# A two-layer graph network on one core: the setup of constants rewritten, sixteen gathers moved into the node pass, and its output rows written in two halves

## The reference, cut to what matters

```python
def _sage_mean(h, src, dst, W_self, W_neigh, b):
    agg = segment_sum(h[src], dst, 50000)
    mean_neigh = agg / maximum(deg, 1.0)[:, None]
    return h @ W_self + mean_neigh @ W_neigh + b
h  = _sage_mean(relu(_sage_mean(x, ..., W_self0, W_neigh0, b0)), ..., W_self1, W_neigh1, b1)
x1 = _layernorm(x + h)
# attention over the edges with q, k + e, v + e (four heads of 128), + x1 @ Wskip + bskip,
# layer norm with ln_g and ln_b, @ Wlin + blin, elu(lin + x1)
x2 = _layernorm(x1 + elu(lin + x1))
```

## Time and profile before

| what | value |
|---|---|
| median of 3 runs | 1757.79 us (1755.62 to 1760.14) |
| the profiled execution, its own time | 1751.26 us |
| its span | 1749.4 us |
| granted TensorE clock, mean of the span | 0.970 |
| PE busy | 1524.3 us (87%) |
| PEld busy | 1024.5 us (59%) |
| DVE busy | 1327.1 us (76%) |
| ACT busy | 1160.0 us (66%) |
| POOL busy | 1041.2 us (60%) |
| DMA | 206.77 MB, mean 118 GB/s |

### The profile page before, as it was taken

How to read it: one execution, slowest core, us unless ns; L and a number is a source line. 1 busy time by engine, 2 the same in 40 slices (tenths; PEclk the granted TensorE clock), 3 DMA queues, 4 the chain that set the end, 5 groups by cost and what they waited for, 6 DMA issues and landing times. The chain is left out here.

```text
span 1749.4 us, 34139 instructions
## 1 busy us (share of the span) xinstructions
PE 1524.3 (87%) x7745; PEld 1024.5 (59%) x7745; DVE 1327.1 (76%) x6197; ACT 1160.0 (66%) x3125; POOL 1041.2 (60%) x1038
## 2 busy tenths in 40 slices
PE   3599999999999998999688867999999999999872
PEld 2477777777777776777455543555555555455441
DVE  4799999999999996656366653777777777777762
ACT  0499999999999995333255541666666666666662
POOL 4688888868888773664455526455555555555320
PEclk9899999999999999999899988999999999999995
DMA  2356566544444442332388853233222232333210
GB/s 79 109 152 158 153 160 154 151 154 144 149 142 148 139 146 74 85 84 70 116 268 271 273 173 80 78 84 85 83 84 84 84 85 79 82 83 85 59 36 4
DMA packets 178820, 206.77 MB, mean 118 GB/s; under 512 B 36607, under 2 KB 104666, under 8 KB 178703
## 3 DMA queue, kind: packets, MB, share of 16 engines
q1 hardware_dynamic: 151502, 169.25, 31.5%
q0 software_dynamic: 27200, 36.26, 9.0%
HBM read 107.47 MB, written 106.49 MB: 122 GB/s over the span
## 5 line engine op out<-in xcount | busy, mean ns | idle before, releaser
L1307 POOL DMA_INDIRECT big<-x_tab,look x196 | 199.6, 1019 | 97.6 <-issue 56.1
L1324 POOL DMA_INDIRECT out_dram<-big,idx x98 | 99.2, 1013 | 259.1 <-DVE big L1640 126.3
L700 PE MATMUL pb<-MG_s,big 128*128 128x256 f32 x832 | 207.4, 392 | 41.5 <-issue 30.7
L700 PEld LDWEIGHTS pb<-MG_s,big 128*128 128x128 f32 x832 | 149.5, 189 | 143.7 <-issue 95.2
L725 ACT ACTIVATE big<-big 128x128 f32<-128x128 f32 x416 | 170.0, 481 | 0.0
L820 POOL TENSOR_TENSOR big<-big,cl 128x512 f32<-128x512 f32 x104 | 133.3, 1282 | 49.8 <-ACT big L749 40.5
L682 PE MATMUL pb<-C_s,big 128*128 128x128 f32 x832 | 161.6, 276 | 0.0
L683 PE MATMUL pb<-Ws1c_s,big 128*128 128x128 f32 x832 | 161.3, 276 | 0.0
L1057 POOL DMA_INDIRECT big<-h1e_tab,hidx x98 | 97.9, 999 | 103.9 <-PE pb L937 45.0
L334 POOL DMA_INDIRECT a_xs<-in_x_dram,idx x98 | 102.3, 1044 | 86.7 <-issue 47.6
L1408 PEld LDWEIGHTS pb<-Wg_s,big 128*128 128x128 f32 x784 | 95.8, 192 | 98.1 <-ACT big L1480 95.8
(11 more groups left out here) (345 smaller groups left out, 4015.1 us busy)
## 6 DMA issues: line engine op xcount, KB each, us to landing
big<-in_x_dram SPq DMA_DIRECT2D x104, 256.0 KB
x_tab<-big SPq DMA_DIRECT2D x98, 256.0 KB
out_dram<-big SPq DMA_DIRECT2D x98, 256.0 KB
ve_tab<-c_ve SPq DMA_DIRECT2D x98, 256.0 KB
c_ve<-ve_tab SPq DMA_DIRECT2D x98, 256.0 KB
h1e_tab<-a_rows SPq DMA_DIRECT2D x25, 256.0 KB
x_tab<-a_rows SPq DMA_DIRECT2D x25, 256.0 KB
big<-eT_tab SPq DMA_DIRECT2D x98, 64.0 KB
```

Source lines behind the costliest of these rows:

```text
L700: t = pe.matmul(o, b_x1T[:, r * P:(r + 1) * P], MG_s[:], start=True, stop=True)
L1307: g.indirect_dma_start(out=o, out_offset=None, in_=x1_tab, in_offset=bass.IndirectOffsetOnAxis(ap=look[:, a, j:j + 1], axis=0), bounds_che ...
```

## The change

Setup: the index rows go out first on SP's queue, the vectors and the larger weights on ACT's queue, and each group has its own semaphore, so that a consumer waits for its group only. The three 256 KB broadcasts of the biases become three rows of 2 KB, which a matmul with a column of 1/D spreads over the partitions. ACT takes the additions of the bias columns, Wg_s, and the copies of Wskip, Wv, Aqk and Aqe out of PSUM from DVE. The PSUM memset goes to the front, and the 10 us memset of POOL behind the last signal that others wait for. Gathers: none in setup and none ahead of the node pass; one in every sixth turn of it (16 in all). Output rows: rows 0 and 1 stay in place, rows 2 and 3 follow the Relu.

```diff
-            for o, i in ((Ws0_s, Ws0), (Wn0_s, Wn0), (Ws1_s, Ws1), (Wn1_s, Wn1), (Wv_s, Wv), (We_s, We),
-                         (Wskip_s, Wskip)):
-                ld(o[:], i)
...
             sp.wait_ge(s_sg, 1)
...
+            ld = load_on(sp, s_li, "index")
             full = NT - 1
             ld(rows_i[0:full, 0, :], dst[0:full * P].rearrange("(t p) -> t p", p=P))
...
-            for o, v in ((set_t, bskip), (set_u, bv), (set_v, be)):
-                ld(o, v.rearrange("(a n) -> a n", a=1).to_broadcast([P, HC]))
...
+            ld = load_on(sp, s_ld, "later")
+            ld(Ws1_s[:], Ws1)
...
+        LOADS = dict(skip=1, lin=1, index=7, rows=10, later=14)
...
+        def setup_act(act):
+            load_on(act, s_lf, "skip")(Wskip_s[:], Wskip)
+            act.preload_act_table_set(ACT_SET)
+            act.wait_ge(s_sg, 1)
+            ld = load_on(act, s_lv, "rows")
+            for r, v in ((18, bskip), (2, bq), (6, bk), (10, bv), (14, be), (22, ln_g), (26, ln_b)):
+                ld(vrow[r:r + 4, :], v.rearrange("(a n) -> a n", n=P))
...
+            ld = load_on(act, s_ld, "later")
+            for r, v in ((0, bskip), (1, bv), (2, be)):
+                ld(set_t[r:r + 1, :], v.rearrange("(a n) -> a n", a=1))
+            ld(set_q, Wq)
...
+            heads_plus(set_sT, 4, 28)
+            w("q")
+            heads_plus(set_qT, 1, 12)
+            w("k")
+            heads_plus(set_kT, 2, 20)
...
+            p("skip")
+            act.activation(Wskip_s[:], pb[6][:], ACT.Copy).then_inc(s_sa, 1)
...
         def setup_pool(g):
...
-            g.wait_ge(s_sg, 7)
-            g.wait_ge(s_sv, vm["idx0"])
-            for s in range(2):
-                gather_src(g, s)
+            g.memset(big[:, b_ghost:b_small_end], 0.0)
...
         def setup_pe(pe):
...
+            pe.matmul(pb[6][:], C_s[:], Wskip_s[:], start=True, stop=False)
+            pe.matmul(pb[6][:], set_one[0:3, :], set_t[0:3, :], start=False, stop=True).then_inc(s_sp, 1)
...
         def b_act(act):
...
-                    for r in range(R):
-                        t = act.activation(b_o[u % 2][:, r * D:(r + 1) * D], b_w[u % 2][:, r * D:(r + 1) * D],
-                                           ACT.Identity, scale=brs3[:, r:r + 1], bias=b_nm3[:, r:r + 1])
-                    t.then_inc(step("b_o"), 1)
+                    for r in range(R // 2):
+                        rows_out(act, u, r)
...
                     act.activation(b_h1T, PH[:], ACT.Relu, bias=b0x[:, 0:1]).then_inc(step("b_h1"), 1)
+
+                    for r in range(R // 2, R):
+                        t = rows_out(act, u, r)
+                    t.then_inc(step("b_o"), 1)
...
         def b_pool(g):
             credit(g, "b_x1c")
-            for s in range(2, 4):
-                gather_src(g, s)
             g.wait_ge(s_red, 16)
...
                     node_row(it)
+                if it % 6 == 5 and it < 96:
+                    gather_src(g, it // 6 // R, it // 6 % R)
```

More of the change, by code:

```diff
@@ L291, in gnn_kernel, with bcast, load_on, ld @@
         s_look = sem("s_look")
-        LOADS = []
+        counts = {n: [] for n in ("skip", "lin", "index", "rows", "later")}
+        def bcast(v, n):
+            return v.rearrange("(a n) -> a n", a=1).to_broadcast([P, n])
+        def load_on(eng, s, what):
+            def ld(o, i):
+                counts[what].append(1)
+                eng.dma_start(o, i).then_inc(s, 16)
+            return ld
         def setup_sync(sp):
@@ new lines, in setup_pe @@
+            pe.wait_ge(s_sg, 3)
+            pe.wait_ge(s_lv, 16 * LOADS["rows"])
+            pe.transpose(pb[0][:, 0:P], vrow, ident[:]).then_inc(s_sp, 1)
+            w("rep1")
+            pe.transpose(pb[7][:, 0:P], rows_f[:, 0, P - 1:P].to_broadcast([P, P]), ident[:]).then_inc(s_sp, 1)
+            for c in range(3):
+                t = pe.transpose(pb[5][:, c * P:(c + 1) * P], rows_f[:, c, :], ident[:])
+            t.then_inc(s_sp, 1)
+            w("sc")
+            four_heads(4, set_sc)
@@ new lines, in setup_pe @@
+            w("vcol")
+            pe.matmul(pb[6][:, 0:H], ones_t, vcol[:, 18:22]).then_inc(s_sp, 1)
+            pe.wait_ge(s_ld, 16 * LOADS["later"])
+            four_heads(1, set_q)
+            four_heads(2, set_k)
+            four_heads(3, We_s[:])
+            a("s")
+            a("wg")
+            sum_heads(pb[0][:, P:2 * P], lambda h: set_sT[:, h, :], lambda h: Wg_s[:, h, :])
+            sum_heads(pb[0][:, 2 * P:3 * P], lambda h: set_sT[:, h, :], lambda h: set_sT[:, h, :]).then_inc(s_sp, 1)
@@ L590, in setup_dve @@
+            v.tensor_tensor(crow[:], pb[7][:, 2 * P:3 * P], set_b[:, D:2 * D], ALU.add)
             v.tensor_scalar(nb0[:], set_b[:, 0:D], -1.0, None, ALU.mult)
-            d("crow", v.tensor_tensor(crow[:], pb[7][:, P:2 * P], set_b[:, D:2 * D], ALU.add))
+            d("cl", v.tensor_tensor(b0x[:], vcol[:, 0:1], pb[7][:, 3 * P:3 * P + 1], ALU.subtract))
+            w("cl")
+            v.wait_ge(s_sa, am["skip"])
+            for b in pb[6:8]:
+                v.memset(b[:].rearrange("p (a d) -> p a d", a=2)[:, :, 0:D], 0.0)
@@ L706, in gnn_kernel, with rows_out @@
         brs1, brs2, brs3 = (b_rs[:, 4 * k:4 * k + 4] for k in range(3))
+        def rows_out(act, u, r):
+            return act.activation(b_o[u % 2][:, r * D:(r + 1) * D], b_w[u % 2][:, r * D:(r + 1) * D],
+                                  ACT.Identity, scale=brs3[:, r:r + 1], bias=b_nm3[:, r:r + 1])
         def b_act(act):
@@ L943, in a_pool @@
                 after(g, "a_pmT", s - 4)
[L944 removed]
+                for r in range(min(R, NT - R * s)):
+                    gather_src(g, s, r)
         def a_dve(v):
```

277 lines of the change are left out of this document (125 added, 152 removed).

## The result

The changed kernel takes 1738.55 us (median of 4 runs, 1737.43 to 1740.29), the kernel before 1756.84 us (4 runs) beside it: ratio 0.9894, 95% interval 0.9877 to 0.9911. That is 18.3 us faster, inside the range of 1717 to 1743 us, though 7.5 us above the 1731 us forecast. The profiled execution took 1740.29 us, its span is 1738.3 us (before 1751.26 and 1749.4).

A forecast was written before the change was run, and what follows sets the result against it. DVE was taken as the bound after the setup's load wait, a PE and ACT ring as the node pass's. Terms -24.3 - 3 - 11.1 + 12 = -26.4 us gave 1725 us profiled, 1731 us against the median; range 1717 to 1743.

The forecast's parts named there:

- The setup: Stage ahead of the node pass: earlier DVE start and shorter DVE chain, end at 30.5 against 54.84 us, -24.3 us.
- DVE's start: Setup: index rows loaded first let DVE start at 12 us instead of 23.15, bounds 10 and 16.
- the third rival: Setup bound by data: DVE starts at 16 us and waits again for later loads, 1737.5 us in all; chance 8%.
- the one-engine rule: Index loads in the setup: 97 partitions would use one DMA engine, putting DVE's start nearer to 14 than 10 us.
- a DVE wait for ACT: Sign that the forecast is wrong: DVE waiting in the setup for ACT, whose copies should hide behind the degrees.
- The start of the node pass: First three turns: with the setup gathers gone POOL is on time and DVE isn't stalled, -3 us.
- The halves: Output rows in two halves shorten the node pass ring; turns fall from 5.871 to DVE's 5.76 us, -11.1 us.
- second rival: The ring doesn't shorten, turns stay at 5.87 us, stalls are partly recovered, gathers cost 10 us: 1740.5 us; chance 17%.
- The gathers: Sixteen gathers in the node pass make x1c late and stall DVE, twelve by 0.6 and four by 1.2: +12 us.
- The rival in which they are absorbed: POOL's slack or shorter waits in its node pass turn take up the gathers: 1719 us; chance 18%.
- x1c out of step: First half of the node pass: POOL's lag never heals, x1c meets L794 every turn, 1.09 us each: 1774 us; chance 4%.
- Stages a, c and d, "untouched": Stages outside setup and node pass: the forecast expected no change in them.

The follow-up runs named there:

- e8: The changed kernel with each load of 97 index rows split into one of 96 and one of 1: 1741.25 us, ratio 0.9916.
- e7: The changed kernel with PE's small products for the degrees ahead of those for Wskip, Wv, Aqk and Aqe: 1735.99 us, ratio 0.9883.
- e4: The kernel before with nothing but the output rows in halves: 1719.59 us, ratio 0.9951.
- e3: The changed kernel with all four output rows ahead of the x1T copy again, gathers unchanged: 1714.13 us, ratio 0.9915.
- e6: The changed kernel with eight gathers in the setup and eight in turns 49 to 51 and 101 to 103: 1727.18 us, ratio 0.9831.
- e10: The same kernel as e6, run once more on the chip of e9: 1724.3 us, ratio 0.9844.
- e2: The changed kernel with its sixteen gathers in turns 49 to 51 and 101 to 103, where POOL has time: 1704.70 us, ratio 0.9867.
- e9: The changed kernel with the edits of e6, e7, e8, degree-row transposes moved up, and the memset in pieces over DVE, ACT and POOL: 1720.38 us, ratio 0.9828.
- e5: The changed kernel once more, no edit, beside the kernel before: 1741.0 us, ratio 0.9902.
- e1: The kernel before once more, no edit, profiled on another chip: 1729.03 us.

## Why the prediction was right, and where it was off

**The setup, -24.3 said, -16.1 measured.** Right in kind: DVE starts on the index rows while the weights still travel, and its chain is shorter. The term was mis-sized by 8.2 us, and outside its bound of 18 at that. Three parts make it up:
- DVE's start, 12 us said, 15.35 measured. The 12 were 1.5 us until SP starts, 8 for the set and 2 for ACT's loads beside it, rounded up. SP started at 1.41 us and the set took 13.9 us from there, so the term for what runs beside it was short by some 4 us. It is the first half of the third rival (a start at 16 us); its second half, a wait of DVE for later loads, didn't come. The forecast said that by the one-engine rule the start would be nearer to 14 than to 10 us, and took 12. e8 settles that the data are late because of the 97-row form: with 96 rows, and ACT's loads beside them as before, they are there at 6.87 us. No run takes ACT's loads away from the 97-row form, so that they are what stretched the set from 8 to 13.9 us is argued, not shown. The Trainium skill ("DMA: Bandwidth & Descriptors", on why a DMA increments its semaphore by 16) says that the number of DMA engines must divide the number of partitions; the trace and e8 agree.
- The cast stood 1.4 us behind POOL's memset (1.75 less 0.36). The forecast had "half a microsecond for meeting POOL's memset" and PE together. It had applied the exclusion in the node pass, from three rows, and not in the setup, where the diff moves a 10 us memset beside the start of the chain.
- The wait of 3.75 us for PE. The forecast checked ACT's sets against the cover of the degrees, but not how much PE has to do, nor in which order: the small products stand behind skip, v, A and Be, and PE works through these without a gap until 33.79 us, when DVE has been ready since 30.07. It named a DVE wait for ACT as a sign of error; it was a wait for PE's own work. e7 puts the small products first, and the wait at L607 is gone; that DVE then stood as long at L633 is for the most part PE's half clock (3.2 of 3.63 us).

Together 3.35 + 1.4 + 3.75 = 8.5 us; the rest of the chain was 0.3 us shorter than said, which leaves the 8.2. The forecast's own sum has a slip in it: 31.7 - 13.6 + 0.4 is 18.5 us, not 18.0, and 19.0 with the half microsecond. Against that the rest of the chain was 0.8 us shorter, so the slip hid half a microsecond of it.

**The start of the node pass, -3 said, -3.05 measured** in the first three turns, and the first load to the first L831 another 0.9 us shorter. Right, mechanism and size: no row of L815 or L835 is stretched in these turns any more, and the halves can't have done it (22.9 us in e4). One row fits the reading only in part: the L774 of 1.97 us in the earlier trace rows starts at 77.49 us, 0.63 us before the addition that it ends with.

**The halves, -11.1 said.** The common turn is 5.76 us as said, with DVE as its bound. Alone (e4) they give 7.7 us on a chip where the turns of before were 5.85. But as a part of this change they are worth about nothing (e3). The two terms aren't additive: the forecast put the 10 us of stalls on top of the shortened ring, and only its second rival said that a stall is partly recovered in a ring that is longer than DVE's work. It is recovered for the most part, 8.5 of 10.4 us. The node pass's 100 turns gained 1.3 us net, where the forecast's terms give -11.1 + 12 = +0.9. That the sum came out right is luck: its two terms were added as if neither touched the other, and the halves' term, a tenth of a microsecond in every turn, was nearly empty beside the gathers.

**The gathers, +12 said, 10.1 measured.** 12 turns of 0.63 and 4 of 1.23 us, where 0.6 and 1.2 were said: this is the step that came out most exactly. The size was 12 x 0.6 + 4 x 1.2 taken in full; the row of 0.15 that each replaces was not taken off, which is the difference (16 x 0.15 = 2.4, less 0.03 us in each of the sixteen). The rival in which they are absorbed fell for this kernel, though with whole rows it nearly holds (1.9 us net in e3), and that of x1c out of step fell too: each stall gave POOL its lag back.

**Stages a, c and d, "untouched".** Not so. The gap behind the pass grew by 5.1 us, which no rival had; 3.76 of them are POOL's longer drain, and e6 and e10 take those away by moving eight gathers out. Stage c's 4.5 us arise around two pauses of PE, whose cause is open, below. All told the traces give -11.1 us and the medians -18.3, against -26.4 said. The 7.2 us between trace and median are the distances of the two profiled executions from their medians; where in the span they arise isn't known.

**The number.** 1738.55 us lies in the range, but nearer to the second and third rivals (1740.5 and 1737.5) than to the forecast's 1731. By the time alone neither could have been told from it; it is the rows that rule them out, the common turns of 5.76 us the one, and the absence of a DVE wait for later loads the other.

## What to carry to other kernels

An engine's slack is read turn by turn, not as a share: a gather of 1.3 us in a turn with 0.3 us of slack costs DVE half a microsecond, and most of the same gathers, in turns with slack or in a stage where POOL idles, cost it nothing (e2, e6), though in the last turns they put off POOL's drain. Before a cost and a gain in the same loop are added up, ask whether the stall gives the ring back what the gain takes from it: here either one made the other invisible (e3, e4). When work is moved past a barrier signal because "nobody waits for it", look at what it shares with those who run beside it; a 10 us memset without a consumer held up the first instruction of the critical chain. And before a run without a gain is taken as proof that an edit is worth nothing, read the granted clock in the stretch where the gain should be: in e7 the products behind the edit ran at half of it.

## What the runs showed of the hardware

- **One DVE copy, 10.24 us.** Beside POOL's memset a DVE cast that takes 0.36 us is stretched to the memset's end (e8). Cut into back-to-back pieces of about 0.9 us, the memset still holds it until the last piece on POOL is over: 2.76 us (e9).
- **97 rows against 96.** With 97 rows in each load, and nothing else moving, the core had about 22 GB/s. As 96 and 1 rows the index rows were there 8.5 us sooner, and SP's queue needed 3.65 instead of 8.95 us to issue them.
- **POOL's drain at the end of a block** takes 3.73 us or 7.49 us, the same to the nanosecond in every kernel of a kind, 4.22 in one.
- **Half the speed at a full clock.** From 24.8 to 26.8 us PE finished 9 products of the setup in e3 and 17 in the kernel after, at a granted clock of 1.00 in both, with the same code.
- **Stage c has two courses.** Counted from PE's first transposes (L1135 in the kernel after) it takes 179.4 to 179.6 us in the kernel after, e5 and e9, and 174.4 to 175.5 us in the ten other profiles. All thirteen come to it behind a pause of PE of 13 us, at a granted clock of 0.50 (the 1.2 GHz level). In the ten the clock stays there for another 5.6 to 7.7 us and then is at 1.00 (2.4 GHz), as in e7:

```profile
839.00:847.00 8.00, 7.31 (x14) 3.41 (x14) 0.93 (x3) 2.20 (x4) 5.80 (x6) 0.51 0.45 136
847.00:863.00 16.00, 15.00 (x79) 10.03 (x78) 10.89 (x43) 8.12 (x19) 8.56 (x9) 1.00 0.77 249
```

In the three it rises within 1.7 us. Yet PE comes to its ninth product with We_s (L1150) no sooner, 10.1 to 10.4 us after the start in the three and 9.5 to 10.4 in the ten. The loss is in the next eight: 10.1 to 10.3 us against 6.0. In the kernel after PE stood still for 2.53 us, and then had 0.50 for some 6 us, in which DVE was busy for 2.44 and POOL for 0.68 us (the stretch 853 to 859 us above):

```profile
851.64 2.71 PE L1150 MATMUL pb<-We_s,a_xs 128*128 128x512 f32 x4 [2.53 <-issue]
855.91 3.78 PE L1150 MATMUL pb<-We_s,a_xs 128*128 128x512 f32 x4 [1.56 <-ACT c_ve L1182]
```

The fallen clock can't be the whole cause. In e5 both pauses stand at a granted clock of 1.00, and it falls only behind them, for 3.4 us (first PE's rows, then stretches with the columns of the earlier trace rows):

```profile
851.90 1.98 PE L1150 MATMUL pb<-We_s,a_xs 128*128 128x512 f32 x4 [2.44 <-issue]
856.24 1.38 PE L1150 MATMUL pb<-We_s,a_xs 128*128 128x512 f32 x2 [2.35 <-ACT c_ve L1182]
...
849.00:855.00 6.00, 2.44 (x9) 0.94 (x7) 0.29 (x2) 0.60 (x1) 3.98 (x4) 1.00 0.47 128
857.00:861.00 4.00, 3.83 (x12) 2.18 (x12) 2.12 (x9) 0.60 (x1) 0.00 (x0) 0.58 0.53 197
```

e7 and e8 differ from the kernel after in the setup alone, so it is no property of the code of stage c, and the three kernels that were profiled twice (before and e1, after and e5, e6 and e10) kept their course. The early rise and the two pauses go together in three of three; what holds PE in the pauses, and what decides when the clock rises, was not tried.
